# Gated cross-attention and expert layers: the expert routing done batch by batch inside the first attention's pipeline

## The chip, the cores and the metric

One core of a Trainium2 chip. The metric is the device time of one execution in microseconds, the median of three runs. The core's engines run their own instruction queues in order and meet through semaphores: TensorE (PE, with its weight loads as PEld), VectorE (DVE), ScalarE (ACT), GpSimd (POOL); SyncE (SP) issues transfers.

## The reference

Two layers on x, 32 batches of 256 rows of 256 numbers, with a context of 120 rows a batch. The change concerns the first attention and the routed feed-forward behind it:

```python
x = x + jnp.tanh(g_xattn[0]) * _L0_xattn_ref(_layernorm(x), ctx, Wq, Wkv, Wo, bo)   # 16 heads, rope
x = x + jnp.tanh(g_ffn[0]) * _L0_ffn_ref(_layernorm(x), w_router, w1, w2, w3)
# _L0_ffn_ref: 8 experts, the best 2 of each row
scores = jax.nn.softmax(xf @ w_router.T, axis=-1)
expert_weights, expert_indices = jax.lax.top_k(scores, 2)
h = silu(xf @ w1[e]) * (xf @ w3[e]);  y = h @ w2[e]      # e: hidden width 352
out = expert_weights[:, 0] * y[first] + expert_weights[:, 1] * y[second]
```

A second attention (with gate and normalised queries) and a ternary feed-forward with a convolution over the rows follow; neither is changed.

## The kernel before

The program is four blocks, one after the other; a block ends when all its engines have ended, and x1 (the rows after the first attention) goes from one to the next through DRAM.

**The first attention** (`attention_first`, L124) is a software pipeline over the 32 batches, written out by hand. `step(at)` is one function for each engine; `at(s)` is the batch that is in stage s in this step, or None. `stepped` (L104) runs the first 8 steps unrolled, then a hardware loop of two steps a turn, then the draining steps; with 6 stages there are 37 steps. Each engine's `step` lists its instructions in a fixed order, with stages mixed: VectorE's begins with a maximum of stage 2, TensorE's with a product of the same stage. Stages: projections, rope and splitting into bf16 halves in 0, turning keys and first maxima in 1, scores, exponentials in 2, values in 3, turning back in 4, the output projection and x1 in 5 (L475, `a_x<-a_ps_b`). A step between two engines goes through a `Signal`, a semaphore counted over batches; `freed` makes TensorE wait for the last reader of a PSUM bank (`ps_a` to `ps_e`, `ps_m`). Splits in two parts: VectorE copies the high halves of keys and queries once more (L439, L497), GpSimd subtracts for the context's low half (L297, `a_cl`).

**The routing and the experts** (`experts`, L1458). Its first part, the routing, takes x1 in 8 groups of 8 row tiles (T = 8). Per group: statistics (L1793), mean and variance (L1799), a power on GpSimd (L1688), the normalised rows (L1808, `e_xn`); TensorE turns them (L1961), ScalarE copies them out (L1746, `e_xf`), TensorE multiplies by the router (L1954); VectorE takes the 8 largest (L1819) and their places (L1824), marks the two experts (L1832), and forms the gates (L1841 to L1849); TensorE counts how many rows before this one chose the same expert (L1984 to L1989), with the counts of earlier groups in `seen`; VectorE turns that into a slot (L1854 to L1865). GpSimd then scatters each row tile to `sent_rows` in DRAM at its slots, once for the first expert and, with the second gate in column 256, once for the second (L1693):

```python
for t in range(T):
    nc.gpsimd.indirect_dma_start(sent[:, :], bass.IndirectOffsetOnAxis(ap=slot[:, g.par, t, k:k + 1], axis=0),
                                 xn[:, g.n % 3, t, :], None).then_inc(sent_k[k][t], 16)
```

Beside it the expert weights are loaded in six pieces and split into bf16 halves (L1737 on ScalarE, L1872 on VectorE, up to 3,072 numbers a partition). Then `tables` (L1887) forms from the counts which expert each of the 71 tiles of 256 slots belongs to, SP fills the slots behind each expert's last with zeros (L1643), and the experts run tile by tile: load (L1655), turn (L1961), products, silu, products, store.

## Time and profile before

| | us |
|---|---|
| median of 3 runs (2208.92 to 2214.29) | 2210.8 |
| the profiled execution | 2211.8 |
| its span, first to last instruction | 2210.0 |
| first attention: first and last x1 write (L475) | 89.6, 482.3 |
| first turn of an expert tile (L1961, `e_xe`) | 756.0 |
| busy over the span: TensorE, VectorE, ScalarE, GpSimd | 1793.5, 1484.0, 1385.6, 1005.0 |

How to read the rows further down. A row of the windows view has the stretch and its length, then busy us and count of instructions for PE, PEld, DVE, ACT and POOL, the granted clock of TensorE (1.00 is 2.4 GHz, 0.50 is 1.2 GHz), the DMA share and GB/s. A row of a group has line, engine, operation, output and inputs, shapes and count, then busy us and the mean duration in ns of one, then the engine's idle us just before these instructions and what ended it. Instructions of one engine overlap at their edges, so the busy time of a group can be under count times mean. A row of the timeline has start and duration in us.

### The profile page before, as it was taken

How to read it: one execution, taken by the hardware profiler on the slowest of the kernel's cores; microseconds unless marked ns; L12 is line 12 of the kernel's file. 1: busy time of each engine (PE TensorE's matmuls, PEld its weight loads, DVE VectorE, ACT ScalarE, POOL GpSimd, SP SyncE). 2: the span in 40 equal slices, each digit the busy share in tenths (PEclk: the TensorE clock that was granted, in tenths of full speed). 3: DMA queues.
4: the chain of work that ended last, by engine and by line, in shares of the span. 5: the costliest groups of instructions: out<-in, count | busy, mean ns of one | idle time of the engine just before them, and what ended most of it. 6: DMA issues, size and time to landing. Idle time of an engine off the chain costs nothing. (4 is left out here: it accounts for less than half of the span.)

```text
span 2210.0 us, 51520 instructions
## 1 busy us (share of the span) xinstructions
PE 1793.5 (81%) x16093; PEld 1493.0 (68%) x16093; DVE 1484.0 (67%) x4076; ACT 1385.6 (63%) x2601; POOL 1005.0 (45%) x1192
## 2 busy tenths in 40 slices
PE   5999999965333399999998189999999648878786
PEld 3777777745323299999998168888888536666665
DVE  4898888846443233323332289999999479999996
ACT  4898888942110144443443177777777449999997
POOL 2444444424666522222222587777776024343332
PEclk8999999985555699999999599999999969999999
DMA  3122222226442323223322445455544201121211
GB/s 105 56 86 85 85 85 85 85 84 212 144 144 81 126 85 90 87 84 90 90 85 75 91 100 124 113 110 115 122 106 99 88 29 58 60 69 57 71 57 48
DMA packets 190731, 202.52 MB, mean 92 GB/s; under 512 B 24912, under 2 KB 180304, under 8 KB 189584
## 3 DMA queue, kind: packets, MB, share of 16 engines
q1 hardware_dynamic: 166032, 166.27, 24.5%
q0 software_dynamic: 24576, 34.62, 7.7%
q8 instruction: 76, 1.25, 0.2%
q14 instruction: 47, 0.39, 0.1%
HBM read 126.59 MB, written 74.24 MB: 91 GB/s over the span
## 5 line engine op out<-in xcount | busy, mean ns | idle before, releaser
L1935 DVE TENSOR_TENSOR e_h<-e_s,e_ps_ab 128x256 f32<-128x256 f32 (+1 forms) x213 | 89.4, 420 | 293.8 <-ACT e_s L1761 293.8
L1726 POOL TENSOR_TENSOR e_h_lo<-e_h 128x256 bf16<-128x256 f32 (+1 forms) x213 | 130.2, 611 | 326.5 <-DVE e_h L1935 326.5
L1954 PE MATMUL e_ps_ab<-e_xt_hi,e_w_hi 128*128 128x256 bf16 (+1 forms) x852 | 233.0, 273 | 0.1
L1954 PE MATMUL e_ps_ab<-e_xt_hi,e_w_lo 128*128 128x256 bf16 (+1 forms) x852 | 232.9, 273 | 0.0
L1954 PE MATMUL e_ps_ab<-e_xt_lo,e_w_hi 128*128 128x256 bf16 (+1 forms) x852 | 232.8, 273 | 0.0
L1693 POOL DMA_INDIRECT sent_rows<-e_xn,e_slot x128 | 140.3, 1096 | 87.1 <-DVE e_seen L1868 48.8
L1761 ACT ACTIVATE e_s<-e_ps_ab 128x256 f32<-128x256 f32 (+1 forms) x213 | 81.5, 383 | 151.5 <-PE e_ps_ab L1954 151.5
L1768 ACT ACTIVATE e_yo<-e_ps_y,e_xe 128x256 f32<-128x256 f32 x142 | 59.7, 471 | 112.6 <-PE e_ps_y L1954 112.6
L2445 PE MATMUL f_ps_h<-f_qh,f_w_q 128*128 128x256 bf16 x512 | 121.6, 279 | 9.3 <-DVE f_y L2347 3.3
L1961 PE MATMUL e_ps_t<-e_ident,e_xn 128*128 128x128 f32 x128 | 33.2, 428 | 110.6 <-DVE e_xn L1808 110.6
L2178 POOL TENSOR_TENSOR f_y<-f_y,f_tmp 128x510 f32<-128x510 f32 x32 | 40.6, 1270 | 181.2 <-DVE f_y L2320 181.2
L2445 PE MATMUL f_ps_h<-f_ql,f_w_q 128*128 128x256 bf16 x512 | 121.6, 279 | 0.0
L1954 PE MATMUL e_ps_y<-e_w_hi,e_h 128*128 (+1 forms) x426 | 116.5, 274 | 0.0
L1954 PE MATMUL e_ps_y<-e_w_hi,e_h_lo 128*128 (+1 forms) x426 | 115.9, 272 | 0.0
L1954 PE MATMUL e_ps_y<-e_w_lo,e_h 128*128 (+1 forms) x426 | 115.7, 272 | 0.0
L960 POOL DMA_INDIRECT a_xa<-back_rows,a_where x64 | 108.2, 1691 | 15.6 <-issue 15.6
L1746 ACT ACTIVATE e_xf<-e_ps_t 128x512 f32<-128x512 f32 x32 | 19.1, 597 | 150.2 <-PE e_ps_t L1961 150.2
L934 POOL DMA_INDIRECT a_xa<-back_rows,a_where x64 | 102.5, 1601 | 16.3 <-issue 16.3
L1961 PEld LDWEIGHTS e_ps_t<-e_ident,e_xn 128*128 128x128 f32 x128 | 27.0, 243 | 111.6 <-DVE e_xn L1808 89.0
L1954 PEld LDWEIGHTS e_ps_ab<-e_xt_hi,e_w_hi 128*128 (+1 forms) x852 | 90.5, 106 | 7.4 <-issue 0.5
L1954 PEld LDWEIGHTS e_ps_ab<-e_xt_lo,e_w_hi 128*128 (+1 forms) x852 | 90.8, 107 | 6.8
L1954 PEld LDWEIGHTS e_ps_ab<-e_xt_hi,e_w_lo 128*128 (+1 forms) x852 | 90.6, 106 | 6.9
(438 smaller groups left out, 6639.6 us busy)
## 6 DMA issues: line engine op xcount, KB each, us to landing
e_xe<-sent_rows SPq DMA_DIRECT2D x71, 272.0 KB, 2.8
back_rows<-e_yo SPq DMA_DIRECT2D x71, 256.0 KB, 2.1
x_rows<-a_x SPq DMA_DIRECT2D x64, 256.0 KB, 2.2
a_xt<-in_xT SPq DMA_DIRECT2D x32, 256.0 KB, 2.9
a_xa<-in_x SPq DMA_DIRECT2D x32, 256.0 KB, 3.7
a_xr<-in_x SPq DMA_DIRECT2D x32, 256.0 KB, 2.8
e_xa<-x_rows SPq DMA_DIRECT2D x8, 1024.0 KB, 10.3
a_xa<-x_rows SPq DMA_DIRECT2D x32, 256.0 KB, 3.2
```

Source lines behind the costliest of these rows:

```text
L934: nc.gpsimd.indirect_dma_start(xa[:, b.par, t, :], None, y_rows[:, :], bass.IndirectOffsetOnAxis(ap=where[:, b.par, 2 * t + 0:2 * t + 1], ...
L960: nc.gpsimd.indirect_dma_start(xa[:, b.par, t, :], None, y_rows[:, :], bass.IndirectOffsetOnAxis(ap=where[:, b.par, 2 * t + 1:2 * t + 2], ...
L1693: nc.gpsimd.indirect_dma_start(sent[:, :], bass.IndirectOffsetOnAxis(ap=slot[:, g.par, t, k:k + 1], axis=0), xn[:, g.n % 3, t, :], None).t ...
L1726: nc.gpsimd.tensor_tensor(h_lo[0:k, b.par, c, :], h[0:k, b.par, c, :], h_hi[0:k, b.par, c, :], ALU.subtract).then_inc(mg.sem, 1)
L1746: nc.scalar.activation(xf[:, q % 2, :, :].rearrange("p k n -> p (k n)"), ps_t[:, q % 2, :], ACT.Copy).then_inc(ra.sem, 1)
L1761: nc.scalar.activation(s[0:k, c, :], ps_ab[0:k, c, 0:N], ACT.Silu).then_inc(ma.sem, 1)
L1768: nc.scalar.activation(yo[:, b.par, t, :], ps_y[:, b.par, t * D:(t + 1) * D], ACT.Copy, scale=xe[:, b.n % 4, t, D:D + 1]).then_inc(my.sem, 1)
L1935: nc.vector.tensor_tensor(h[0:k, b.par, c, :], s[0:k, c, :], ps_ab[0:k, c, N:2 * N], ALU.mult).then_inc(mh.sem, 1)
L1954: last = nc.tensor.matmul(to, left, right, start=(i == 0), stop=(i == len(terms) - 1))
L1961: last = nc.tensor.transpose(to[:, c * N + t * P:c * N + (t + 1) * P], rows_[:, t, c * P:(c + 1) * P], ident[:, :])
L2178: nc.gpsimd.tensor_tensor(y[:, 0:2, 0:N - 1], y[:, 0:2, 0:N - 1], tmp[:, 0:2, 0:N - 1], ALU.add).then_inc(gp3.sem, 1)
L2445: last = nc.tensor.matmul(dst, l, r, start=(n == 0), stop=(n == len(terms) - 1))
```

## The change

- **Stages.** The routing of a batch (2 row tiles) becomes stages 7, 8 and 9 of the first attention's pipeline, which has 10 stages and so 41 steps, 12 unrolled first. Projections, rope and splitting move from stage 0 to 1, most others of the front by one stage too; x1 stays in stage 5. All five queues are laid out in a new order, and PSUM banks are given out anew.
- **Per step, from the routing:** all of the work told above, for 2 row tiles instead of 8, reading x1 from SBUF instead of DRAM. The normalised rows are made on ScalarE (scale and a negative mean times rstd), the difference before the exponential, `both` and `seen` on GpSimd. The bases of the experts are added by a product (`base_part`) instead of by VectorE; maxima read PSUM directly. Two scatters for the first expert, two for the second. VectorE puts the second gate in place once the first scatters have landed. Slots go to DRAM (`slots`).
- **Moved between engines:** the copies of the high halves go from VectorE to ScalarE, the context's low half from GpSimd to VectorE.
- **Expert weights:** four of the six pieces are split inside the attention (`also`, steps 1 to 8), the last two at the start of the experts. The stores of zeros to the spare rows are in step 6.
- **Experts:** start with the count, the tables and the padding; the final places are worked out after tile 4 from the slots read back.

```diff
-            stepped(eng, step, 6, 8)
+            filled(eng, step, 10, 12, also)
+def filled(eng, step, stages, fixed, also):
...
+    for n in range(fixed):
+        step(at(n))
+        also(n)
...
 # SP
+                b = at(9)
+                if b is not None:
+                    dve8.wait(sp, b, "eslf")
+                    nc.sync.dma_start(slots[b.n], slot[:, b.par, :, :].rearrange("p t k -> p (t k)")).then_inc(s_st[b.par], 16)
...
+                    dve1.wait(sp, at(2), "cl")
+                    nc.sync.dma_start(ca[:, b.par, :, :], a["ctxT"][b.n]).then_inc(c_ld[b.par], 16)
...
+                if n in (4, 5):
+                    sh.load(sp, a, n - 2)
+                if n == 6:
+                    for j in range(SPARE // ROWS):
+                        at = E * ROOM + j * ROWS
+                        sp.dma_start(sent[at:at + ROWS, :].rearrange("(t p) d -> p t d", p=P), sh.zeros[:, :, :]).then_inc(sh.s_spare, 16)
 # GpSimd, first in its step
+                b = at(9)
+                if b is not None:
+                    g0.wait(gp, at(10), "paced")
+                    dve8.wait(gp, b, "ecol0")
+                    nc.gpsimd.tensor_tensor(pace_g0[:, :], half[:, 0:1], half[:, 0:1], ALU.mult).then_inc(g0.sem, 1)
+                    for t in range(NT):
+                        nc.gpsimd.indirect_dma_start(sent[:, :], bass.IndirectOffsetOnAxis(ap=slot[:, b.par, t, 0:1], axis=0),
+                                                     e_xn[:, b.par, t, :], None).then_inc(e_sent[0][t][b.par], 16)
...
+                    dve9.wait(gp, b, "ecol1")
...
+                    nc.gpsimd.tensor_tensor(seen[:, :], seen[:, :], more[:, :], ALU.add).then_inc(gp9.sem, 1)
...
+                    nc.gpsimd.tensor_tensor(both[:, :, :], is_k[:, 0, :, :], is_k[:, 1, :, :], ALU.add).then_inc(gp8.sem, 1)
 # ScalarE
+                    dve7.wait(act, b, "enm")
+                    for t in range(NT):
+                        last = nc.scalar.activation(e_xn[:, b.par, t, 0:D], x1[:, b.par, t, :], ACT.Identity, bias=e_nmr[:, t:t + 1], scale=e_rstd[:, t:t + 1])
...
+                    nc.scalar.activation(kx[0:S, :, 64:96], kx[0:S, :, 0:32], ACT.Copy).then_inc(act1.sem, 1)
...
+                    nc.scalar.activation(qx[:, :, :, 32:64], qx[:, :, :, 0:32], ACT.Copy).then_inc(act1.sem, 1)
+            def also(n):
...
+                if n in (1, 2):
+                    sh.high(nc, n - 1, sh.flat[0])
+                if n in (6, 7):
+                    sh.high(nc, n - 4, sh.flat[1])
 # VectorE
-                    nc.vector.tensor_copy(kx[0:S, :, 64:96], kx[0:S, :, 0:32])
-                    nc.vector.tensor_copy(qx[:, :, :, 32:64], qx[:, :, :, 0:32])
+                    nc.vector.tensor_tensor(cl[:, :, :], ca[:, b.par, :, :], ch[:, :, :], ALU.subtract).then_inc(dve1.sem, 1)
...
+                        last = nc.vector.max(top[:, t, :], ps_d[:, t * E:(t + 1) * E])
...
+                        last = nc.vector.max_index(which[:, t, :], top[:, t, :], ps_d[:, t * E:(t + 1) * E])
...
+                b = at(9)
+                if b is not None:
+                    landed(dve, e_sent[0][0], b)
+                    landed(dve, e_sent[0][1], b)
+                    nc.vector.tensor_copy(e_xn[:, b.par, :, D:D + 1], pair[:, b.par, :, 1:2]).then_inc(dve9.sem, 1)
...
+                    nc.vector.tensor_tensor(found[:, :, :, :], is_k[:, :, :, :].rearrange("p k t e -> p t k e"),
+                                            ps_c[:, 0:NT * E].rearrange("p (t e) -> p t e", e=E).unsqueeze(2).to_broadcast([P, NT, 2, E]), ALU.mult).then_inc(dve8.sem, 1)
...
+                if n in (2, 3):
+                    sh.low(nc, n - 2, sh.flat[0])
+                if n in (7, 8):
+                    sh.low(nc, n - 5, sh.flat[1])
 # TensorE
+                    last = transposed(ps_d, e_xn[:, b.par, :, :])
...
+                        last = product(ps_d[:, t * E:(t + 1) * E], [(e_xf[:, c, t * P:(t + 1) * P], router[:, c, :]) for c in range(KC)])
...
+                    nc.tensor.matmul(ps_c[:, 0:NT * E], below[:, :], both[:, :, :].rearrange("p t e -> p (t e)"), start=True, stop=False)
+                    nc.tensor.matmul(ps_c[:, 0:NT * E], ones[:, :], base_part[:, :], start=False, stop=False)
+                    nc.tensor.matmul(ps_c[:, E:NT * E], ones[:, :], both[:, 0, :], start=False, stop=False)
+                    for t in range(NT):
+                        last = nc.tensor.matmul(ps_c[:, t * E:(t + 1) * E], ones[:, :], seen[:, :], start=False, stop=(t == NT - 1))
 # experts
+                if b.n == 4:
+                    places_()
...
+                if b.n == 1:
+                    pe.wait_ge(sh.s_low, 6)
```

## Rows read from the trace of the kernel before

**Rows 1.** Lines view of the x1 write (L475), in 100 to 450 and whole.
```profile
L475 DVE SCALAR_TENSOR_TENSOR a_x<-a_ps_b,a_tg,a_xb x26: 741/743/751, 102.7 to 441.0; 128x512 f32<-128x512 f32 x26
...
L475 DVE SCALAR_TENSOR_TENSOR a_x<-a_ps_b,a_tg,a_xb x32: 741/743/752, 89.6 to 482.3; 128x512 f32<-128x512 f32 x32
```

**Rows 2.** Timeline of the two handovers: start us, us, engine, line, what.
```profile
485.74 0.36 SPq L1614 DMA_DIRECT2D e_ident<-in_ident  x1
...
716.66 0.19 PE L2001 MATMUL e_ps_y<-e_seen,e_ones 128*128 128x8 bf16 x1 [11.05 <-DVE e_seen L1868]
...
718.23 9.31 SPq L1643 DMA_DIRECT2D sent_rows<-e_zeros  x8
...
753.02 3.88 SPq L1655 DMA_DIRECT2D e_xe<-sent_rows  x4
...
756.02 1.09 PE L1961 MATMUL e_ps_t<-e_ident,e_xe 128*128 128x128 f32 x4 [39.18 <-DMA e_xe<-sent_rows]
```

**Rows 3.** Windows view, ten steps of the first attention: busy us of each engine.
```profile
165.02:299.92 134.90, 131.49 (x1268) 100.42 (x1272) 120.65 (x317) 120.22 (x219) 59.59 (x70) 1.00 0.28 87
```

**Rows 4.** Groups of VectorE in those ten steps.
```profile
L499 DVE SCALAR_TENSOR_TENSOR a_qx<-a_qf,a_rstd,a_qx 128x256 bf16<-128x256 f32 x20 | 8.8, 480 | 0.0
L464 DVE COPY a_q<-a_mt 32x2048 bf16<-32x2048 bf16 x10 | 8.7, 874 | 11.2 <-ACT a_mt L346 11.2
...
L440 DVE TENSOR_TENSOR a_kx<-a_kf,a_kx 120x256 bf16<-120x256 f32 x9 | 3.7, 414 | 0.0
...
L497 DVE COPY a_qx<-a_qx 128x512 bf16<-128x512 bf16 x10 | 2.8, 283 | 0.0
...
L457 DVE MEMSET a_tick<- 128x1 f32 x10 | 0.6, 59 | 0.0
```

**Rows 5.** Groups of ScalarE in those ten steps.
```profile
L370 ACT ACTIVATE a_qx<-a_qf,a_rstd 128x256 bf16<-128x256 f32 x20 | 9.0, 499 | 0.4 <-POOL a_qf L299 0.2
L319 ACT ACTIVATE a_xh<-a_xt 128x512 bf16<-128x512 f32 x10 | 6.3, 630 | 2.2 <-DMA a_xt<-in_xT 1.9
...
L322 ACT ACTIVATE a_ch<-a_ca 128x240 bf16<-128x240 f32 x10 | 4.0, 403 | 10.3 <-DMA a_ca<-in_ctxT 10.3
```

**Rows 6.** Groups of GpSimd and ScalarE in the routing, 485 to 765.
```profile
L1693 POOL DMA_INDIRECT sent_rows<-e_xn,e_slot x128 | 140.3, 1096 | 87.1 <-DVE e_seen L1868 48.8 <-issue 32.7 <-DMA sent_rows<-e_xn,e_slot 3.3
...
L1746 ACT ACTIVATE e_xf<-e_ps_t 128x512 f32<-128x512 f32 x32 | 19.1, 597 | 150.2 <-PE e_ps_t L1961 150.2
```

**Rows 7.** Timeline of the routing around one scatter.
```profile
572.62 3.08 DVE L1872 TENSOR_TENSOR e_w_lo<-e_w_f,e_w_hi 128x2816 bf16<-128x2816 f32 x1
573.12 3.50 POOL L1693 DMA_INDIRECT sent_rows<-e_xn,e_slot  x1 [5.47 <-DVE e_seen L1868]
...
576.92 0.96 POOL L1693 DMA_INDIRECT sent_rows<-e_xn,e_slot  x1 [0.30 <-issue]
```

**Rows 8.** Groups of VectorE in the routing, 485 to 765.
```profile
L1793 DVE BATCH_NORM_STATS2 e_stats<-e_xa 128x6 f32<-128x256 f32 x64 | 21.6, 412 | 3.8 <-DMA e_xa<-x_rows 3.8
...
L1872 DVE TENSOR_TENSOR e_w_lo<-e_w_f,e_w_hi 128x2816 bf16<-128x2816 f32 x4 | 12.3, 3084 | 0.0
L1824 DVE FIND_INDEX8 e_which<-e_top,e_logits 128x8 uint32<-128x8 f32 x64 | 8.9, 160 | 0.0
...
L1799 DVE BATCH_NORM_AGGREGATE e_mv<-e_stats 128x2 f32<-128x6 f32 x64 | 5.1, 153 | 0.2
...
L1846 DVE SCALAR_TENSOR_TENSOR e_pair<-e_ex,e_tg,e_rec 128x16 f32<-128x16 f32 x8 | 1.9, 235 | 0.3
```

**Rows 9.** Groups of TensorE in the first attention, 100 to 450.
```profile
L542 PEld LDWEIGHTS a_ps_b<-a_wo,a_ot 128*128 128x128 f32 x208 | 37.5, 190 | 4.0
...
L552 PE MATMUL a_ps_a<-a_ident,a_of 128*128 128x128 f32 x104 | 15.6, 273 | 0.0
```

**Rows 10.** Groups of GpSimd in the ten steps.
```profile
L295 POOL TENSOR_TENSOR a_rstd<-a_ve,a_half 128x2 f32<-128x2 f32 x10 | 7.8, 776 | 0.8
...
L297 POOL TENSOR_TENSOR a_cl<-a_ca,a_ch 128x240 bf16<-128x240 f32 x10 | 7.3, 730 | 0.0
```

More of the change, by code:

```diff
@@ new lines, in filled, with at, within @@
+def filled(eng, step, stages, fixed, also):
+    def at(n):
+        return lambda s: Batch(n - s, (n - s) // 2, (n - s) % 2) if 0 <= n - s < B else None
+    def within(batch):
+        return lambda s: batch.back(s) if s else batch
+    for n in range(fixed):
+        step(at(n))
+        also(n)
+    with eng.Fori(0, (B - fixed) // 2) as k:
+        step(within(Batch(2 * k + fixed, k + fixed // 2, 0)))
+        step(within(Batch(2 * k + fixed + 1, k + fixed // 2, 1)))
+    for n in range(B, B + stages - 1):
+        step(at(n))
@@ L125, in attention_first @@
+def attention_first(nc, sem, a, src, dst, sh, sent, slots):
     tag = "a0_"
@@ L183, in attention_first @@
         ch, cl = [sb(n, [P, KC, S], BF16) for n in ("ch", "cl")]
+        tick1, tick2, tick3 = [sb(f"tick{i}", [P, 1], F32) for i in (1, 2, 3)]
+        numbers = sb("numbers", [P, E], F32)
+        router = sb("router", [P, KC, E], F32)
+        below_f = sb("below_f", [P, P], F32)
+        below = sb("below", [P, P], BF16)
+        e_stats = sb("e_stats", [P, NT, 6], F32)
+        e_mv = sb("e_mv", [P, NT, 2], F32)
+        e_ve, e_rstd, e_nmr, total, e_rec = [sb(n, [P, NT], F32) for n in ("e_ve", "e_rstd", "e_nmr", "total", "e_rec")]
+        e_xf = sb("e_xf", [P, KC, N], F32)
+        top, drop, e_ex = [sb(n, [P, NT, E], F32) for n in ("top", "drop", "e_ex")]
+        base_part = sb("base_part", [P, NT * E], BF16)
+        which = sb("which", [P, NT, E], mybir.dt.uint32)
+        pair = sb("pair", [P, 2, NT, 2], F32)
+        is_k = sb("is_k", [P, 2, NT, E], F32)
+        both = sb("both", [P, NT, E], BF16)
+        found = sb("found", [P, NT, 2, E], F32)
+        more = sb("more", [P, E], F32)
         ps_a, ps_b, ps_c, ps_d = [psum(f"ps_{i}", [P, 512]) for i in "abcd"]
@@ L396, in _ @@
+            run(nc.scalar, step, also)
         @block.vector
@@ new lines, in step @@
+                b = at(9)
+                if b is not None:
+                    nc.vector.tensor_reduce(more[:, :], both[:, :, :].rearrange("p t e -> p e t"), AX_X, ALU.add).then_inc(dve9.sem, 1)
+                b = at(7)
+                if b is not None:
+                    dve7.wait(dve, b, "ebn")
+                    nc.vector.memset(tick1[:, :], 0.0)
+                    for t in range(NT):
+                        last = nc.vector.bn_aggr(e_mv[:, t, :], e_stats[:, t, :])
+                    last.then_inc(dve7.sem, 1)
@@ new lines, in step @@
+                b = at(8)
+                if b is not None:
+                    landed(dve, s_st, at(10))
+                    dve8.wait(dve, b, "efound")
+                    with nc.allow_low_precision(reason="slots are whole numbers"):
+                        last = nc.vector.tensor_reduce(slot[:, b.par, :, :], found[:, :, :, :], AX_X, ALU.add)
+                    last.then_inc(dve8.sem, 1)
+                    nc.vector.tensor_copy(e_xn[:, b.par, :, D:D + 1], pair[:, b.par, :, 0:1]).then_inc(dve8.sem, 1)
@@ L1522, in experts @@
-        total = sb("total", [P, T], F32)
-        rec = sb("rec", [P, T], F32)
-        pair = sb("pair", [P, 2, T, 2], F32)
-        is_k = sb("is_k", [P, 2, T, E], F32)
-        both = sb("both", [P, T, E], BF16)
-        place = sb("place", [P, T, E], F32)
-        found = sb("found", [P, T, 2, E], F32)
-        slotf = sb("slotf", [P, GR, T, 2], F32)
-        slot = sb("slot", [P, 2, T, 2], I32)
-        more = sb("more", [P, E], F32)
-        seen = sb("seen", [P, E], BF16)
+        ident, bases, ends, tri, iota, starts, ones, seen = sh.ident, sh.bases, sh.ends, sh.tri, sh.iota, sh.starts, sh.ones, sh.seen
```

1270 lines of the change are left out of this document (619 added, 651 removed).

## The prediction

> **What bounds the kernel now.** I read the windows first: the program is one chain of four programs, so a stretch counts by its length. The first attention writes its last x1 at 482.3 to 483.1 [rows 1], the routing runs from there to 756.0, where the first expert tile is turned [rows 2]; the experts and both later parts follow and are not touched. So the question is what the first 756.0 us become.
>
> Inside the attention, x1 is written every (441.0 - 102.7)/25 = 13.5 us [rows 1]. In ten such steps TensorE is busy 131.5 of 134.9 us, VectorE 120.7, ScalarE 120.2, GpSimd 59.6 [rows 3]: 13.15, 12.07, 12.02 and 5.96 us a step. Three engines have at most 1.4 us a step free, so work moved in isn't free. VectorE's idle time is 1.12 us a step before the copy of the shifted maxima (L464), waiting for ScalarE [rows 4]; ScalarE's is 1.03 us before L322, waiting for a load [rows 5]. In the routing stretch no engine is near full: it is a chain of waits from group to group, with 128 scatters on GpSimd, 140.3 us, plus 0.3 us between two [rows 6, 7].
>
> **What is removed.** All from 483.1 to 756.0: 272.9 us. Some comes back at its end (the tables, the padding stores, the first load).
>
> **What a step gets.** Instructions of VectorE overlap: the 27 groups of ten steps, L499 to L457, sum to 138 us [rows 4] against 120.7 of busy time in 317 instructions [rows 3], so 0.056 us each. Per batch of two row tiles VectorE gets two statistics at 21.6/64 = 0.34, two aggregations and two maxima at 0.08 and two index searches at 0.14 [rows 8], three small memsets: about 1.5 us. Then ten single small ones (is_k, found, slot, more, pair, total, reciprocal, the negative mean, two gate columns); the pair takes 0.235 [rows 8], and I take 0.2 for each: 2.0. Then the remainder of the context, from GpSimd, as L440, 0.41 [rows 4]. Out go two bf16 copies, the larger 0.28 [rows 4], together 0.5. Durations: 1.5 + 2.0 + 0.4 - 0.5 = 3.4; minus 0.056 x 16 it is 2.5. VectorE: 12.1 + 2.5 = **14.6 us**. Ends: 2.0 (the small ones at 0.15) and 3.4 (no overlap).
>
> ScalarE gets the normalised rows as one more pair like L370, 9.0/10 = 0.9 [rows 5]; the routing's turned rows, 0.60 [rows 6]; an exponential of 16 numbers, taken as 0.2 (at most the 0.40 of L322); the two copies from VectorE: 0.40 as L322 and 0.63 as L319 [rows 5]. Sum 2.7, less overlap 0.3: 12.0 + 2.4 = **14.4 us**.
>
> TensorE gets four f32 turns at 15.6/104 = 0.15, four router products, each bound by its f32 weights, 37.5/208 = 0.18 [rows 9], and five count products that are smaller still, 0.2 together: 1.5. **14.6 us**, or 14.2 if the modelled ends overstate it by the part that the weight loads cover. The granted clock is 1.00, the level of 2.4 GHz, through the ten steps [rows 3]; TensorE's share would go from 0.97 to 0.94, so I keep it.
>
> GpSimd gets four scatters, 0.96 alone plus 0.30 to the next [rows 7]: 5.0; one power at 0.78 for one subtraction of 0.73 that leaves [rows 10]; six small instructions at about 0.2: 1.2. 6.0 + 6.3 = **12.3 us**. A scatter can be held: the one at 573.12 took 3.50 us, for it ran until 0.9 us after VectorE's 3.08 us subtraction of two SBUF operands had ended [rows 7]. A step has some 2.6 us of such subtractions and of plain copies; if each of the four scatters meets the worst of them, a pair like L499, 8.8/10 = 0.9 [rows 4], GpSimd reaches 12.3 + 4 x 0.9 = 15.9. I take 13.
>
> The Trainium skill (SBUF — State Buffer, Who interferes with whom) says that a tensor_tensor of two SBUF inputs takes only the read side, so that descriptor writing should go on beside it; the trace disagrees, with that 3.50 us. By the page the scatters would stay at 0.96 and GpSimd at 12.3.
>
> So the three full engines stand at 14.4 to 14.6. Before, the step was 1.03 times TensorE's busy time and 1.12 times VectorE's. By the first a step becomes 15.0, by the second 16.3. The new stages have their inputs a step ahead, the two waits above get other work ahead of them (1.0 us of it before L464), and against this three queues must fit instead of one. I take **15.5**; ends 14.7 (the busiest engine alone) and 16.5.
>
> **The sum to the first expert tile.**
> - To the first x1: 89.6 before [rows 1]. The first step loses its products (stage 0 to 1), and x1 is written later in VectorE's step (past three quarters, before under half): about -7 and +6. I keep 89.6, plus or minus 8.
> - Weights: four of the six pieces are split inside the attention, 3.08 us each on VectorE [rows 8]. Two fall into full steps (7, 8), two into the idle filling steps, where I count half: 9.
> - Steps 5 to 31: 26 x 15.5 = 403.
> - Drain. Five steps took 482.3 - 441.0 = 41.3 [rows 1]; with 2 us more each, 51. Then four steps with routing alone, which is a chain: two scatters 2.5, landing 2.5 (a load's landing by [rows 2] is 3.0), gate column 0.2, two scatters 2.5, both 0.2, ranks 0.6, found, slot and column 0.7, and handovers of about 0.2 each: 10.5 us a step, 42 to 44. Together 95. Ends 75 and 115.
> - Handover: to the next block's first instruction 2.7 (483.1 to 485.74), count and padding 1.6, eight padding stores 9.3, landing 3.0, first load to first turn 3.0 [rows 2]: 19.6. The tables (716.65 to 722, small instructions of VectorE) and the last two pieces, 6.2 by [rows 8], end inside it; with no cover left the pieces cost those 6.2.
>
> 89.6 + 9 + 403 + 95 + 19.6 = 616 instead of 756.0: 140 less. The final places, five instructions on up to 1,024 numbers a partition, are worked out after tile 4, about 4.5 us of VectorE (1,024 numbers at a third of the 3.08 us for 2,816, each); TensorE then has one tile's products ahead, so I count 2 (ends 0 and 4.5). The seven stores of zeros now stand in SP's queue in step 6, 7 x 9.3/8 = 8 us by the padding's stores [rows 2], with the loads of step 7 behind them; SP is ahead by half a step, so I count nothing; uncovered it is those 8. The small store of slots in each step waits on VectorE's slot of the step before, and only the x1 store and the context's load stand behind it. Net **-138**: 2211.8 - 138 = **2074 us** against the profiled execution's 2211.8, 1.0 above the median of the runs, 2210.8, which is under what counts here.
>
> **The rivals.**
> *A, the balanced step (0.62):* a step of 14.7 to 16.5. 26 steps move it by -21 to +26, the drain by 10 more: 2045 to 2105.
> *B, GpSimd as the bound (0.20):* with scatters held (15.9 us of work) and in-order waits between them on VectorE's gate column, a step of 17.0 to 18: 2074 + 26 x 1.5 to 2.5 = 2113 to 2139. For it: the held scatter. Against it: 128 scatters average 1.10 [rows 6], and 26 of 31 VectorE instructions in a step aren't of the holding kind.
> *C, better than the work suggests (0.14):* the drain's steps stay near 8 us, and the first steps are shorter: 2025 to 2045. For it: five drain steps took 8.3 each before.
> *D, slower than before (0.03):* the gate column (ecol1) stands in VectorE's queue some 3.8 us into a step and waits for two scatters to land; everything behind it on VectorE waits too. The first column is written at about 10.6 us of the step before, so there are 15.5 - 10.6 + 3.8 = 8.7 us for scatters and landing, which need 1.3 + 2.5 and a handover: 4 us to spare. It decides only if it lengthens every step by over 138/26 = 5.3 us, so GpSimd has to come 9.6 us late. By the queue orders it has some 2.5 us of waiting left in each step. Price at that point: 2211.
> *E, nothing gained (0.01):* B and D together bring the step to 20.5 to 21.1 us; within 0.3% means 2204 to 2218.
>
> 0.3% (6.6 us) is about what a measurement of this kernel can tell from no change. A, B and C are faster: 0.96; E 0.01; D 0.03. Range: A, and B's nearer half and C's nearer half, 2040 to 2125.
>
> **What the profile will show.** Starts of the x1 write (the fused multiply-add after the projection) 15.5 us apart, clock 1.00 there; VectorE, ScalarE and TensorE over 90% busy, GpSimd 75 to 85%; scatters at 0.96 to 1.9 us, mean 1.2; the last scatter at about 597; the first turn of an expert tile at 616; experts, second attention and last part as long as before. I am wrong first in the step: at over 16.5 one engine's queue waits on another in every step, and the chain of waits will name it (gate column or the count product). I am wrong in the drain if its last four steps aren't near 10 us each.

## The result and the profile after

The changed kernel takes 2107.91 us (median of 4 runs, 2106.21 to 2113.87) against 2211.36 for the kernel before beside it: a ratio of 0.9536, 95% interval 0.9514 to 0.9559. It is faster by 103 us. I forecast 2074, 138 less; the time lies inside the range of 2040 to 2125. The profiled execution took 2108.9, so 34.9 us of the forecast are missing.

First, the writes of x1 (the timeline of VectorE: start, duration, engine, line, operation, and in brackets the idle time before it and what ended it). They answer to [rows 1].

```profile
95.11 0.75 DVE L820 SCALAR_TENSOR_TENSOR a_x<-a_ps_b,a_tg,a_xb 128x512 f32<-128x512 f32 x1 [0.42 <-PE a_ps_b L866]
...
257.02 0.75 DVE L820 SCALAR_TENSOR_TENSOR a_x<-a_ps_b,a_tg,a_xb 128x512 f32<-128x512 f32 x1
...
417.50 0.75 DVE L820 SCALAR_TENSOR_TENSOR a_x<-a_ps_b,a_tg,a_xb 128x512 f32<-128x512 f32 x1
...
529.80 0.75 DVE L820 SCALAR_TENSOR_TENSOR a_x<-a_ps_b,a_tg,a_xb 128x512 f32<-128x512 f32 x1
...
596.24 0.75 DVE L820 SCALAR_TENSOR_TENSOR a_x<-a_ps_b,a_tg,a_xb 128x512 f32<-128x512 f32 x1 [2.71 <-PE a_ps_b L866]
```

Ten steps lie between 257.02 and 417.50: 16.05 us each. The nine steps before them take 161.9 us, 17.4 more than 9 x 16.05. The timeline of the handover follows, as in [rows 2].

```profile
633.26 0.96 POOL L453 DMA_INDIRECT sent_rows<-k_xn,k_slot  x1 [0.30 <-issue]
...
638.55 8.73 SPq L1885 DMA_DIRECT2D sent_rows<-k_zeros  x8
...
652.97 1.09 PE L2049 MATMUL e_ps_t<-k_ident,e_xe 128*128 128x128 f32 x4 [15.87 <-DMA e_xe<-sent_rows]
```

The first expert tile is turned at 653.0, not at 756.0: here are the 103 us. What follows lasts 2107.1 - 653.0 = 1454.1 us; before it was 2210.0 - 756.0 = 1454.0. That these agree to 0.1 us is partly luck: in eight of the runs below, which leave that part as it is here, it lasts 1455.0 to 1461.8.

| stretch | forecast | measured | difference |
|---|---|---|---|
| start to the first x1 | 89.6 | 95.1 | +5.5 |
| 26 steps at their steady length | 403 | 417.3 | +14.3 |
| weights and slow filling steps | 9 | 17.4 | +8.4 |
| x1 of step 31 to the last scatter's end | 95 | 104.4 | +9.4 |
| handover | 19.6 | 18.7 | -0.9 |
| after the first turn (the places) | 2 | 0.1 | -1.9 |

The steady stretch by windows (busy us and instructions of PE, PEld, DVE, ACT, POOL, then granted clock, DMA share, GB/s), beside [rows 3]:

```profile
257.02:417.50 160.48, 145.56 (x1452) 116.36 (x1451) 159.26 (x540) 142.97 (x281) 113.13 (x171) 1.00 0.35 108
```

Per step that is TensorE 14.56, VectorE 15.93, ScalarE 14.30, GpSimd 11.3. The sums of TensorE (14.6) and ScalarE (14.4) hold. GpSimd's 12.3 counted the pauses between scatters, 0.8 us a step in the waits view, which its busy time leaves out; with them it is at 12.1, and the 13 that I took was too high. VectorE, forecast at 14.6, is busy 99% of the time. Its groups in this stretch (busy us, mean ns):

```profile
L769 DVE SCALAR_TENSOR_TENSOR a_e_nmr<-a_e_mv,a_e_rstd 128x2 f32<-128x2 f32 x10 | 12.8, 1285 | 0.0
L673 DVE TENSOR_TENSOR a_cl<-a_ca,a_ch 128x240 bf16<-128x240 f32 x10 | 11.5, 1152 | 0.0
...
L773 DVE SCALAR_TENSOR_TENSOR a_pair<-a_e_ex,a_tg,a_e_rec 128x4 f32<-128x4 f32 x10 | 6.5, 648 | 0.0
```

A negative mean of 128x2 numbers takes 1.29 us. I had put it at 0.2, and the context's remainder at the 0.41 of L440 [rows 4]. The timeline of one step shows what lies beside it:

```profile
363.65 0.48 DVE L648 TENSOR_TENSOR a_k_sin<-a_ps_a,a_sin 120x128 f32<-120x128 f32 x2
364.04 0.65 DVE L764 TENSOR_REDUCE a_mneg<-a_ps_m 128x4 f32<-128x480 f32 x1
...
364.39 0.72 POOL L475 TENSOR_TENSOR a_kf<-a_k_cos,a_k_sin 120x256 f32<-120x256 f32 x1
364.61 1.81 DVE L769 SCALAR_TENSOR_TENSOR a_e_nmr<-a_e_mv,a_e_rstd 128x2 f32<-128x2 f32 x1
365.08 1.26 POOL L476 TENSOR_TENSOR a_qf<-a_rc,a_rs 128x512 f32<-128x512 f32 x1
...
366.35 0.21 DVE L773 SCALAR_TENSOR_TENSOR a_pair<-a_e_ex,a_tg,a_e_rec 128x4 f32<-128x4 f32 x1
366.48 0.65 DVE L778 TENSOR_REDUCE a_mneg<-a_ps_m 128x4 f32<-128x480 f32 x1
...
367.18 0.38 PE L1014 MATMUL a_ps_m<-a_k,a_q 96*128 96x240 bf16 x2 [1.35 <-DVE a_mneg L778]
```

GpSimd sums the rotated keys (kf) and queries (qf) until 366.34. The negative mean, begun at 364.61, ends at 366.42. The maximum behind it comes late by as much, and TensorE waits 1.35 us for it. The waits of TensorE and GpSimd over 258 to 417 (total, times, longest):

```profile
POOL a_pace_g L430 <- DVE k_xn L804: 16.3, 10, 1.7
POOL a_pace_g L451 <- DVE k_xn L725: 16.2, 10, 1.6
...
PE a_ps_m L1014 <- DVE a_mneg L778: 12.6, 10, 1.4
```

GpSimd waits 1.6 us twice a step: it isn't the bound (rival B). The scatters average 1.17 us at L432 and 1.02 at L453. VectorE waited twice for sent rows at its gate column, 2.5 us in a filling step and 4.6 us at the end of the drain, and in no steady step (rival D).

### The profile page after: what moved, and what is told of

Its sections match the earlier page's. It is cut to its first block and busy times, and to the rows that moved or that the text cites. A ratio compares the mean times of both kernels' runs of the same rounds, so it can differ in the third digit from the quotient of the medians.

```text
span 2107.1 us, 52385 instructions
## 1 busy us (share of the span) xinstructions
PE 1764.3 (84%) x16125; PEld 1465.1 (70%) x16125; DVE 1515.6 (72%) x4237; ACT 1435.4 (68%) x2754; POOL 1012.3 (48%) x1358
## 5 line engine op out<-in xcount | busy, mean ns | idle before, releaser
L2042 PE MATMUL e_ps_ab<-e_xt_hi,k_w_hi 128*128 128x256 bf16 (+1 forms) x852 | 233.2, 274 | 0.2 <-DVE e_xt_lo L2019 0.2
L2042 PE MATMUL e_ps_ab<-e_xt_lo,k_w_hi 128*128 128x256 bf16 (+1 forms) x852 | 233.0, 273 | 0.0
L2042 PE MATMUL e_ps_ab<-e_xt_hi,k_w_lo 128*128 128x256 bf16 (+1 forms) x852 | 232.9, 273 | 0.0
L1308 POOL DMA_INDIRECT a_xa<-back_rows,a_where x64 | 108.4, 1694 | 16.0 <-issue 15.7
L2042 PEld LDWEIGHTS e_ps_ab<-e_xt_hi,k_w_hi 128*128 (+1 forms) x852 | 90.7, 106 | 7.5 <-issue 0.6
L2042 PEld LDWEIGHTS e_ps_ab<-e_xt_lo,k_w_hi 128*128 (+1 forms) x852 | 90.8, 107 | 6.7
L2042 PEld LDWEIGHTS e_ps_ab<-e_xt_hi,k_w_lo 128*128 (+1 forms) x852 | 90.7, 106 | 6.9
L432 POOL DMA_INDIRECT sent_rows<-k_xn,k_slot x64 | 71.3, 1114 | 20.3 <-issue 20.3
L453 POOL DMA_INDIRECT sent_rows<-k_xn,k_slot x64 | 65.4, 1022 | 18.2 <-issue 15.1
L1314 POOL TENSOR_TENSOR a_xl<-a_xt,a_xh 128x512 bf16<-128x512 f32 x32 | 37.5, 1171 | 66.5 <-ACT a_xh L1372 66.5
L2527 PE MATMUL f_ps_p<-f_ident,f_zm 128*128 128x128 f32 x256 | 34.9, 279 | 38.5 <-ACT f_zm L2264 38.5
```

Source lines behind the costliest of these rows:

```text
L1308: nc.gpsimd.indirect_dma_start(xa[:, b.par, t, :], None, y_rows[:, :], bass.IndirectOffsetOnAxis(ap=where[:, b.par, 2 * t + 1:2 * t + 2], ...
L2042: last = nc.tensor.matmul(to, left, right, start=(i == 0), stop=(i == len(terms) - 1))
```

## The experiments

Three theories went in. T1: small VectorE instructions on SBUF tiles are held while GpSimd works on SBUF tiles, and this lengthens the step. T2: VectorE only has more work of its own. T3: GpSimd or the order of waits sets the step. All runs in one table (first x1, steady step over ten steps, first turn of an expert tile, from the profiled execution; ratio to the kernel before, with interval):

| run | first x1 | step | first turn | ratio |
|---|---|---|---|---|
| the changed kernel | 95.1 | 16.05 | 653.0 | 0.9536 [0.9514, 0.9559] |
| 1 negative mean, one tile | 97.0 | 15.31 | 640.8 | 0.9471 [0.9454, 0.9488] |
| 2 context's remainder on GpSimd | 96.9 | 15.71 | 643.5 | 0.9467 [0.9452, 0.9483] |
| 3 splits in the drain | 95.6 | 15.97 | 650.7 | 0.9506 [0.9485, 0.9527] |
| 4 more work on GpSimd | 95.6 | 15.93 | 645.5 | 0.9507 [0.9491, 0.9523] |
| 5 changed kernel again | 93.2 | 15.97 | 649.4 | 0.9527 [0.9511, 0.9543] |
| 6 mean and pair, one tile | 96.4 | 15.97 | 653.8 | 0.9524 [0.9507, 0.9541] |
| 7 as 6, with 2 | 94.9 | 15.89 | 649.9 | 0.9505 [0.9490, 0.9521] |
| 8 splits in the handover | 95.0 | 15.97 | 635.7 | 0.9483 [0.9467, 0.9498] |
| 9 mean and pair moved | 96.8 | 20.44 | 732.8 | 0.9678 [0.9619, 0.9736] |
| 10 as 9, with 8 | 95.8 | 20.43 | 695.4 | 0.9778 [0.9713, 0.9842] |
| 11 GpSimd waits for the pair | 96.8 | 14.95 | 624.0 | 0.9390 [0.9368, 0.9412] |
| 12 as 11, with 8 | 93.7 | 14.93 | 614.5 | 0.9391 [0.9374, 0.9407] |

The groups of runs 1 to 4, 5 to 8 and 9 to 11 each ran on one chip, beside the same runs of the kernel before; run 12 had its own. The two runs of the changed kernel differ by 3.6 us at the first turn; smaller differences say nothing. Ratios are of several executions, the other columns of one, so the two need not agree to a few us.

**1. The negative mean with one tile as input.**

```diff
-  nc.vector.scalar_tensor_tensor(e_nmr[:, :], e_mv[:, :, 0], -1.0, e_rstd[:, :], ALU.mult, ALU.mult)
+  for t in range(NT):
+      last = nc.vector.tensor_scalar(e_nmr[:, t:t + 1], e_mv[:, t, 0:1], e_rstd[:, t:t + 1], -1.0, ALU.mult, ALU.mult)
```

> The negative mean times 1/std (128x2, 1285 ns in the steady step of the changed kernel, 160 ns in the drain) is written as two tensor_scalar instructions of VectorE, each with one tile as input and the 1/std as a per-partition scalar; the same values, on the same engine, at the same place. Theory T1 (VectorE instructions with two SBUF tiles as inputs are held while GpSimd works on SBUF tiles; VectorE bounds the step): the two take under 200 ns together, the step falls from 16.05 us by about 1.0 to about 15.0, 26 steps give 24 to 28 us, time about 2082. Rival T2 (this instruction waits for its input, or is slow for its own reason, and VectorE merely has more work): the time of the pair stays about 1.2 us and the total within 0.3% of 2108. Rival T3 (GpSimd, not VectorE, sets the step): VectorE gets idle time of 1 us per step and the total stays.

The two instructions take 0.33 us together, and the hold went to the next one, the pair of gates. The timeline of VectorE, pair and x1 write in three steps:

```profile
265.93 1.38 DVE L775 SCALAR_TENSOR_TENSOR a_pair<-a_e_ex,a_tg,a_e_rec 128x4 f32<-128x4 f32 x1
270.09 0.75 DVE L822 SCALAR_TENSOR_TENSOR a_x<-a_ps_b,a_tg,a_xb 128x512 f32<-128x512 f32 x1
281.75 1.57 DVE L775 SCALAR_TENSOR_TENSOR a_pair<-a_e_ex,a_tg,a_e_rec 128x4 f32<-128x4 f32 x1
286.09 0.75 DVE L822 SCALAR_TENSOR_TENSOR a_x<-a_ps_b,a_tg,a_xb 128x512 f32<-128x512 f32 x1
297.73 0.28 DVE L775 SCALAR_TENSOR_TENSOR a_pair<-a_e_ex,a_tg,a_e_rec 128x4 f32<-128x4 f32 x1
...
300.78 0.75 DVE L822 SCALAR_TENSOR_TENSOR a_x<-a_ps_b,a_tg,a_xb 128x512 f32<-128x512 f32 x1
```

With the pair at 1.57 us the step from 270.09 is 16.00 long, with 0.28 the next is 14.69. So it goes in all ten steps: five with the pair at 1.34 to 1.57 take 15.84 to 16.02 us, five with 0.22 to 0.28 take 14.69 to 14.74, and TensorE waits for the maximum behind the pair in five steps, 5.5 us in all. In the free case shown the pair is done within 0.1 us of the start of GpSimd's qf (297.95); in the held ones it ends when qf ends. My size for T1 (15.0 in every step) was wrong. Hold and step go together; that the hold is the cause is not shown here, but in run 11.

**2. The context's remainder back on GpSimd** (its place in VectorE's step is deleted, the waits of SyncE and TensorE go to GpSimd's signal).

```diff
+  act0.wait(gp, b, "ch")
+  nc.gpsimd.tensor_tensor(cl[:, :, :], ca[:, b.par, :, :], ch[:, :, :], ALU.subtract).then_inc(gp1.sem, 1)
```

> The low half of the context (128x240, 1152 ns on VectorE in the changed kernel) goes back to GpSimd, behind the low half of the batch. VectorE loses 1.15 us per step, GpSimd gains about 0.45 to 0.9 us and stands at about 12 us per step. T1 and any theory in which VectorE bounds the step: step 15.0 to 15.2, total about 2083 to 2088; by T1 part may come back, since GpSimd then holds the port longer under other instructions of VectorE (bn_stats and copies not, two-tile ones yes). T3 (GpSimd or the order of waits bounds): same or slower, since GpSimd's later work comes later by 0.5 to 0.9 us.

VectorE loses 1.2 us of busy time a step (147.43 in 157.08 us), the step only 0.34, to 15.71 where I had expected 15.0 to 15.2. The pair is held in each step, 1305 ns on average. That no engine's busy time explains the step was new: TensorE 14.5 us, VectorE 14.7, in a step of 15.71.

**4. More work on GpSimd.**

```diff
   nc.gpsimd.tensor_tensor(qf[:, :, :], rc[:, :, :], rs[:, :, :], ALU.add).then_inc(gp1.sem, 1)
+  nc.gpsimd.tensor_tensor(qf2[:, :, :], rc[:, :, :], rs[:, :, :], ALU.add).then_inc(gp1.sem, 1)
```

Not shown: the two waits that keep the second sum from being overwritten too early. Neither appears among the waits of the steady stretch.

> GpSimd repeats the sum of the rotated queries (two SBUF tiles, 1.26 us) into a tile that nothing reads: 1.26 us more of GpSimd per step, 12.6 of 16 us. T1: VectorE's instructions with two SBUF tiles beside it get longer (negative mean from 1.29 towards 2.5 us, or the low halves of keys and queries, whichever lies beside it); step 16.3 to 17.2, total 2115 to 2138. T2: VectorE's durations stay; total within 0.3%. T3 (GpSimd's own length sets the step): the step grows by the whole 1.26 us, 2141, and VectorE has idle time in it.

GpSimd is busy 1.25 us more a step (windows, steady stretch):

```profile
252.33:411.64 159.31, 145.98 (x1452) 116.44 (x1451) 151.97 (x540) 144.22 (x280) 125.60 (x181) 1.00 0.36 109
```

The step stays at 15.93. T3 falls: GpSimd has slack of over 1.25 us. But T1 in my form (more GpSimd work, longer holds) fell too, though this edit tests it weakly: in one step the added sum begins at 313.23, just before the pair ends (313.28), and beside it stand maxima, which keep their 0.65 us. The hold merely sits elsewhere, at the pair (1302 ns) and not at the negative mean (412), and VectorE's busy time of 15.2 us is no longer the step. So "VectorE is 99% busy, hence the bound" was a misreading: its busy time contains the hold, and the step is a circuit. A small instruction of VectorE is held until qf ends; the maximum behind it is late; TensorE, in order, waits 1.1 us for it in each step (1.3 in the changed kernel), and VectorE later waits 0.5 us for TensorE (the turned sums, L1067 there).

**3 and 8. The weight pieces' splits elsewhere.** In 3 the splits of pieces 2 and 3 move from steps 6 to 8 to steps 32 to 34, in 8 to the start of the experts, and those of pieces 4 and 5 behind the first tile's hidden layer (the pieces are numbered from 0). The loads of pieces 4 and 5 move along: in 3 from steps 9 and 10 to 34 and 35, in 8 behind the loads of the first four tiles. The edit of 3 on ScalarE (VectorE's and SyncE's are alike; in 8 the same calls stand at the start of the experts):

```diff
-                if n in (6, 7):
-                    sh.high(nc, n - 4, sh.flat[1])
+                if n in (B, B + 1):
+                    sh.high(nc, n - B + 2, sh.flat[1])
```

> The splits of the third and fourth weight piece, and the loads of the fifth and sixth, move from the filling steps 6 to 10 to the draining steps 32 to 35. If the slow filling steps (20.2, 22.4 and 18.3 us against 16.05) come from these splits, they fall to about 16.5 to 17: 8 to 11 us less before the steady steps. In the draining steps VectorE and ScalarE have idle time (the chain of routing sets 10.7 to 12.3 us each), so the splits (3.07 and 2.54 us) cost 0 to 4 us there; a rival says that they delay the drain's chain by their full length, 6 to 10 us, and nothing is won. Then the last pieces' split may be late for the second expert tile, cost 0 to 5. Forecast 2097 to 2104; nothing won: 2108.

> The splits of the third and fourth weight piece move from the filling steps into the handover to the experts (in which TensorE waits about 16 us for the first tile's rows), those of the fifth and sixth behind the first expert tile's hidden layer. The pieces' move to the draining steps gained 14 us in the filling steps and lost 13.6 us in the draining steps. Here the filling steps gain the same 14 us, the draining steps stay at 12 to 14 us, and the handover is a rival's place for the loss: two splits of 3.07 us stand in front of the first tile's low half, 0 to 4 us; the fifth and sixth piece may come late for the first down product, 0 to 8 us. Forecast 8 to 14 us under the control; nothing won if the later splits cost as much as the earlier ones.

In the changed kernel the two low halves take 3.07 and 5.06 us in steps of 20.2 and 22.4. The longer one is held too. It starts beside two instructions of GpSimd on SBUF tiles, of which the second ends at 153.29, and ends 2.96 us after that; TensorE then waits 4.37 us behind it, and the granted clock averages 0.85 in this step:

```profile
150.91 1.27 POOL L438 TENSOR_TENSOR a_xb<-a_xr,a_bias 128x512 f32<-128x512 f32 x1
151.19 5.06 DVE L186 TENSOR_TENSOR k_w_lo<-k_w_f,k_w_hi 128x2816 bf16<-128x2816 f32 x1
152.13 1.16 POOL L442 TENSOR_TENSOR a_xl<-a_xt,a_xh 128x512 bf16<-128x512 f32 x1
...
158.87 1.09 PE L914 MATMUL a_ps_d<-a_identb,a_qx 128*96 128x128 bf16 x8 [4.37 <-DVE a_which L691]
```

Without the two splits the first nine steps take 147.3 us (run 8) against 160.8 in run 5: the 13.5 us are real (some 4 of them are a step of 20.0 us, two behind the last split, that run 8 doesn't have; runs 1, 2, 4, 6, 7 and 11 have the splits but not this step, and what it is stands under run 9). In the drain they cost it all again: the steps behind the x1 write of 529.8 of 13.7, 12.1 and 12.4 us become 18.4, 17.0 and 16.0. My 0 to 4 us was wrong; that the chain of the drain has idle time on VectorE and ScalarE did not help. In the handover they cost nothing up to the first turn (13.7 us earlier than in run 5), but the next waits of TensorE (605 to 760) show the bill:

```profile
PE e_ps_t L2051 <- DMA e_xe<-sent_rows: 16.0, 2, 15.7
PE e_ps_y L2054 <- PEq L210: 11.2, 1, 11.2
PE e_ps_y L2044 <- DVE e_w_lo L186: 6.9, 1, 6.9
```

The first down product waits 6.9 us for the low half of the last piece. The part behind the first turn lasts 1467.8 us, in run 5 1457.3, so 10.5 of 13.7 us are given back in this pair of executions (over all runs that part lasts 1454.1 to 1461.8 us with these splits in the pipeline or the drain, and 1467.2 to 1467.9 in runs 8, 10 and 12). The ratio of 0.9483 against 0.9527 (intervals just apart) is what is left.

**5. The changed kernel again.** 

> The changed kernel itself once more, as the neighbour of the next three on the same chip. Ratio to the kernel before as measured: 0.9514 to 0.9559; every theory expects steady steps of about 16.0 us.

Confirmed. In this execution the negative mean takes 769 ns and the pair 1083, other than in the first profile (1285 and 648), but together they are as long (1.85 and 1.93 us). VectorE is busy 15.33 us a step in place of 15.93, and the step is the same. The 0.6 us are the context's remainder: 546 ns here, 1152 there, 392 in run 9. It is held too, by GpSimd's batch remainder (`a_xl`), and ends 0.28 us after it. This hold costs the step at most 0.1 us, other than the one ahead of the maximum.

**6 and 7. The pair too as tensor_scalar; with the context's remainder on GpSimd.**

```diff
-  nc.vector.scalar_tensor_tensor(pair[:, b.par, :, :], e_ex[:, :, 0:2], tg[:, 1:2], e_rec[:, :].unsqueeze(2).to_broadcast([P, NT, 2]), ALU.mult, ALU.mult)
+  for t in range(NT):
+      last = nc.vector.tensor_scalar(pair[:, b.par, t, :], e_ex[:, t, 0:2], tg[:, 1:2], e_rec[:, t:t + 1], ALU.mult, ALU.mult)
```

> The negative mean and the pair of gates (128x4), the two small instructions of VectorE that stand with two SBUF tiles as inputs in front of the maximum that TensorE waits for, are both written as two tensor_scalar instructions with one tile as input and per-partition scalars. In the run that did so for the negative mean alone the hold moved to the pair: steps in which the pair took 1.34 to 1.57 us were 15.84 to 16.02 long, steps in which it took 0.22 to 0.28 were 14.7 long. T1 with a circuit (the hold delays the maximum, and TensorE, which waits for it 1.5 us per step, is the real bound at 14.6): every steady step 14.7 us, TensorE without wait there; about 34 us under the control, about 2075. A rival says that the steps of 15.9 have a cause of their own that also lengthens the pair (a slow GpSimd or transfer): then 14.7 and 15.9 go on alternating and the gain stays at 12 to 15 us.

> As the run without holds, and the context's low half back on GpSimd. VectorE alone as the bound: step 14.7 less up to 0.5 us. TensorE as the bound at 14.6 (my theory): no gain over the run without holds, both within 0.2% of each other; GpSimd busier by 0.8 us per step.

Nothing gained, against my forecast of 34 us. The groups of VectorE in run 6 say why:

```profile
L776 DVE TENSOR_SCALAR a_pair<-a_e_ex,a_tg,a_e_rec 128x2 f32<-128x2 f32 x20 | 15.4, 815 | 0.0
...
L770 DVE TENSOR_SCALAR a_e_nmr<-a_e_mv,a_e_rstd 128x1 f32<-128x1 f32 x20 | 3.2, 201 | 0.0
```

The pair is held in the new form as well, 1.5 us for its two instructions, although each streams one tile and takes the others as one number a partition. Those of one number a partition (128x1) aren't, beside GpSimd's kf. So two tiles as inputs is not the whole condition. The Trainium skill (SBUF — State Buffer, Who interferes with whom) says that a VectorE instruction with two SBUF inputs contends with a GpSimd instruction that reads SBUF; the trace agrees (1285 ns against 148 in run 11). The Trainium skill says there too that copies, casts and tensor_scalar can enter two-port modes, when their operands meet certain conditions, and can then contend with GpSimd; the trace agrees for the 128x2 numbers. The Trainium skill also says there that a tensor_reduce never contends on this chip, and the maxima beside GpSimd's sums stay at 0.64 us here; but they read PSUM, so this is no test of a reduction of SBUF.

**9 and 10. The two moved ahead in VectorE's order; with the splits in the handover.** The pair goes ahead of the keys' rotation, the negative mean behind it, ahead of the maximum of ms1. Nothing else changes in run 9.

> Only VectorE's order changes. The pair of gates moves ahead of the keys' rotation, the negative mean directly behind it, ahead of the maximum of ms1: GpSimd can't begin the keys' and queries' sums (0.72 and 1.26 us) before the keys' rotation is done, so these two small instructions stand beside short GpSimd work or get the port first. T1 as the earlier runs left it (it is not the two tiles of the negative mean alone; whichever small instruction of VectorE follows the start of the queries' sum on GpSimd is held until it ends, and TensorE waits behind the maximum that follows): pair and negative mean under 0.5 us each, no wait of 1.4 us before TensorE's product for the maximum, steps of 14.7 us in place of 15.95, first expert turn 30 to 34 us earlier than in the control (649.4), total 2075 to 2085. Rival (the hold goes on to the next instruction, or the steps of 15.95 have another cause): steps stay at 15.9 and the total within 0.3% of 2108.

> The order of the run before, with the weight pieces' splits in the handover as in the run that had them there (which brought the first expert turn from 649.4 to 635.7). If both gains stand beside each other: steady steps 14.7 us, first expert turn at about 603, total 2060 to 2072. If the filling steps and the steady ones share one cause, it is the gain of one of them alone, 2075 to 2095.

The holds are gone (pair 189 ns, negative mean 147), and the kernels are slower than the changed one: 2153 us with a spread of 2130 to 2194, and 2167 with 2152 to 2182. Nearly every steady step takes 20.4 us. Slices of one step of run 9 by windows:

```profile
306.00:307.00 1.00, 1.00 (x14) 0.79 (x12) 1.00 (x1) 1.00 (x3) 0.98 (x2) 1.00 0.85 198
307.00:308.00 1.00, 0.04 (x1) 0.00 (x0) 1.00 (x1) 1.00 (x4) 1.00 (x2) 1.00 0.61 222
308.00:309.00 1.00, 0.00 (x0) 0.00 (x0) 1.00 (x1) 1.00 (x2) 0.84 (x1) 1.00 0.00 0
309.00:310.00 1.00, 0.25 (x2) 0.24 (x3) 1.00 (x4) 1.00 (x2) 0.00 (x0) 0.93 0.00 0
310.00:311.00 1.00, 1.00 (x7) 1.00 (x6) 1.00 (x4) 0.34 (x1) 0.00 (x0) 0.50 0.92 214
...
315.00:316.00 1.00, 1.00 (x11) 0.28 (x4) 0.00 (x0) 0.14 (x1) 0.70 (x2) 0.50 0.00 0
316.00:317.00 1.00, 1.00 (x15) 1.00 (x14) 0.00 (x0) 0.84 (x3) 0.98 (x2) 0.66 0.38 139
```

TensorE stands still for 2.7 us, then the granted clock is at 0.50 (1.2 GHz) for some 6 us. The timeline shows what holds what:

```profile
309.75 0.53 PE L1084 MATMUL a_ps_m<-a_k,a_q 96*128 96x240 bf16 x2 [2.71 <-DVE a_mneg L832]
...
314.15 0.60 ACT L513 ACTIVATE a_raw<-a_ps_e 128x512 f32<-128x512 f32 x1 [3.81 <-PE a_ps_e L893]
...
317.91 0.69 DVE L736 COPY a_q<-a_mt 32x2048 bf16<-32x2048 bf16 x1 [3.08 <-ACT a_mt L529]
```

TensorE waits for VectorE's maximum; its products behind the gap run at half the clock; ScalarE waits 3.8 us for them; the turned maxima come late, VectorE waits 3.1 us for them, and its maximum is late again in the next step. In the slices before the gap the clock is 1.00, so the gap comes first. The sum closes as well: TensorE is busy 17.69 us a step here against 14.71 in run 11, for the same 1452 matmuls in ten steps, and 17.7 + 2.7 = 20.4. Run 10's trace shows the same gap:

```profile
308.32 0.38 PE L1078 MATMUL a_ps_m<-a_k,a_q 96*128 96x240 bf16 x2 [2.71 <-DVE a_mneg L828]
```

Read this way, the form feeds itself; no run broke the circle to test it. In run 10 the fourth to eighth step (without splits and holds) take 14.3 to 15.5 us, and from the ninth on 20.4; near the end three of 15.2 to 16.0 come between them. The spread of the times would fit executions that differ in how many steps are of this form; only one of each is read here, for run 9 the slowest of its four. I had forecast 2075 to 2085 for run 9 and 2060 to 2072 for run 10, and nothing of this. The new order isn't what starts such a step: the filling has single ones elsewhere, in the changed kernel (19.64 us), in run 5 (20.0) and in run 12 (20.13), each with a gap before the same maximum and the clock at 0.50 behind it, and the step after it takes 15.0 to 16.1 us. The gaps in the changed kernel and in run 12, and the windows view of run 12's step:

```profile
210.08 0.38 PE L1084 MATMUL a_ps_m<-a_k,a_q 96*128 96x240 bf16 x2 [3.12 <-DVE a_mneg L832]
...
210.80 0.38 PE L1080 MATMUL a_ps_m<-a_k,a_q 96*128 96x240 bf16 x2 [2.41 <-DVE a_mneg L830]
```

```profile
205.97:226.10 20.13, 17.67 (x145) 13.33 (x145) 16.39 (x55) 14.41 (x29) 10.09 (x16) 0.83 0.28 80
```

Only with the new order does it go on from step to step. Why it dies out in the old one, and which of the two moves matters, was not tried.

**11. GpSimd waits for the pair.** VectorE's order stays.

```diff
   dve1.wait(gp, b, "rope_k")
+  if at(8) is not None:
+      dve8.wait(gp, at(8), "epair")
   nc.gpsimd.tensor_tensor(kf[0:S, :], k_cos[0:S, :], k_sin[0:S, :], ALU.add).then_inc(gp1.sem, 1)
```

> VectorE's order as in the changed kernel; GpSimd waits, before the keys' sum, until VectorE has done the pair of gates. So no GpSimd instruction over 0.2 us can stand beside the negative mean and the pair. T1: the two take 0.16 and 0.22 us, the maximum that TensorE waits for comes 1.1 to 1.5 us earlier in each step, the keys' and queries' sums about 0.9 us later; steps 14.7 us if nothing waits for the sums, up to 15.4 if ScalarE's copies of them come late. Rival (another cause of the 15.95): 15.95 or more, since only a wait was added.

One added wait makes the kernel 1.4% faster than the changed one: 2082.68 us, ratio 0.9390. The step of 14.95 is inside what I expected. Timeline and windows of the steady stretch:

```profile
304.55 0.15 DVE L771 SCALAR_TENSOR_TENSOR a_e_nmr<-a_e_mv,a_e_rstd 128x2 f32<-128x2 f32 x1
304.62 0.21 DVE L775 SCALAR_TENSOR_TENSOR a_pair<-a_e_ex,a_tg,a_e_rec 128x4 f32<-128x4 f32 x1
304.75 0.65 DVE L780 TENSOR_REDUCE a_mneg<-a_ps_m 128x4 f32<-128x480 f32 x1
304.91 0.73 POOL L477 TENSOR_TENSOR a_kf<-a_k_cos,a_k_sin 120x256 f32<-120x256 f32 x1 [0.55 <-DVE a_pair L775]
```

```profile
262.92:412.39 149.47, 147.08 (x1452) 115.57 (x1450) 145.49 (x541) 141.94 (x282) 112.93 (x171) 1.00 0.39 116
```

The step is 14.95 us, with TensorE busy 14.71 of it, and the waits view of these ten steps shows no wait of a matmul (in the changed kernel 12.6 us in ten steps, for the maximum alone): now TensorE is the bound. VectorE's busy time is 14.55, the forecast's sum, and the context's remainder is still held in it (1071 ns). The first turn comes 25.4 us before that of run 5; 26 steps of 1.02 us are 26.5. This settles T1 in its last form: the hold by kf and qf costs the steady step 1.0 us, and neither VectorE's amount of work (T2) nor GpSimd's (T3) sets it. The fourth to eighth step of run 10, in which another edit takes the same two holds away, are as short.

**12. Both gains.**

> GpSimd waits for the pair of gates before the keys' sum (alone: steps of 14.95 us, ratio 0.9390), and the splits of the third and fourth weight piece stand in the handover (alone: first expert turn 13.7 us earlier, ratio 0.9483 beside a control of 0.9527). If the two gains add: filling steps 15 to 16.5 us, steady steps 14.95, first expert turn at about 609 to 612, total 2066 to 2074, ratio 0.932 to 0.936. Rival: the faster filling ends in the other regime that the two reordered kernels fell into (a gap of TensorE of 3 us, the granted clock at 0.5 behind it, steps of 20.4 us, kept up by themselves); then total over 2130.

All three forecasts were missed. The first turn is at 614.5 (forecast 609 to 612), 9.5 us ahead of run 11, and the time is the same (2084.13 us, ratio 0.9391; forecast 2066 to 2074, 0.932 to 0.936). Five us of the filling went into the one step of 20.13 shown above. TensorE waits 8.3 us for the low half of the last piece at the first down product, and the part behind the first turn takes 1467.9 us in place of 1461.8. Run 11 or 12 is the best version of this study; to keep its gain, 12 would need the last two pieces earlier (not tried).

## Why the prediction was right, and where it was off

- *The place and the size of the gain.* Right in kind: all of it lies before the first expert tile, nothing changed behind it, and three nearly full engines and GpSimd (70%) take the routing in. 103 of 138 us came. The 2107.9 lie in the range but in no rival's span: A ends at 2105 (by its own terms, 2074 + 26 + 10, at 2110), B begins at 2113.
- *The engines' sums.* Right: TensorE 14.56 (14.6), ScalarE 14.30 (14.4), GpSimd 12.1 with its pauses (12.3, taken as 13). VectorE is at 14.55 in run 11 (14.6), but partly by luck: this contains a hold of 0.7 us on the context's remainder, which I had priced at 0.41, so the rest was too high by as much. I also took off the overlap for 16 more instructions a step; there are 22 more (540 in ten steps against 317).
- *The step of 15.5.* This term failed: 16.05, which makes 14.3 of the 34.9 us. I had set it by ratios of step to busy time, "0.2 for each" of the small instructions of VectorE among the terms. I looked for the hold on the wrong side: the argument was that VectorE's long instructions hold GpSimd's scatters. These are hardly held (1.17 and 1.02 us against 0.96). GpSimd's sums hold VectorE's smallest instructions, two of which stand right ahead of the maximum that TensorE waits for (runs 1, 4, 6, 11). Without this hold the step is 14.95, in the lower half of rival A's steps. That the time came out inside the range is owed to the range's width: nearly all terms erred the same way.
- *Weights and filling steps, 9 us.* They took 17.4. Shown: the two splits in full steps cost 13.5 us (run 8), where I had put about 6, for VectorE alone. I left out that a split can be held as well (5.06 us for one), that TensorE waits behind it (4.37 us) and then runs at a lower clock, and that ScalarE has 2.5 us of high half in a nearly full step of its own; some 4 us are the single step with the gap. How the rest divides among these wasn't tried. Most of the remaining 4 is the third step, which takes 19.2 us in run 8 too.
- *The first x1 at 89.6.* It came at 95.1, and at 93.2 to 97.0 in the other runs; inside the 8 us that I allowed. Nothing was tried on it.
- *The drain, 95 us.* 104.4. The four steps with routing alone took 38.0 (forecast 42 to 44, so the chain was priced 4 to 6 us too high, 9.5 us a step in place of 10.5). This hid part of the other error: the five steps before took 66.4 in place of 51: I had given them 2 us each, and they are 11.4 to 16.9 us long, which looks like the routing's chain already bounding them. Run 3 shows that they have no room: a split adds itself.
- *The tables, the last pieces and the zeros at nothing, the places at 2.* The first three hold. The part with the places is 0.1 us longer than before, but it varies by up to 7.7 us between runs, so their 2 us can't be told from nothing.
- *Rival B* did not come: a wait of 1.6 us twice a step is left to GpSimd. *Rival D* did not either: waits of 2.5 and 4.6 us, outside the steady steps. What could have taken up to half of the gain is one that I did not name: the circuit of runs 9 and 10, one reordering away.
- *The signs.* VectorE and TensorE are over 90% busy, as I wrote; ScalarE is at 89% and GpSimd at 70% (75 to 85 forecast), the scatters' mean is 1.09 us (1.2), and the last scatter starts at 633 (597).
